# Starting a second attention with all rows of the first batch, and its loads in another order

## The reference

```
def _L1_xattn_ref(x, y, wq, bq, wk, bk, wv, bv, wo, bo):      # y: context, 8 x 120 x 384
    q = (x @ wq + bq).reshape(B, SQ, 16, 32)                  # x: layer norm of the rows
    k = (y @ wk + bk).reshape(B, SKV, 16, 32)
    v = (y @ wv + bv).reshape(B, SKV, 16, 32)
    scores = jnp.einsum('bqhd,bkhd->bhqk', q, k) / jnp.sqrt(32)
    attn = jax.nn.softmax(scores, axis=-1)
    out = jnp.einsum('bhqk,bkhd->bqhd', attn, v).reshape(B, SQ, 512)
    return out @ wo + bo
x = x + jnp.tanh(g_xattn[1]) * _L1_xattn_ref(_layernorm(x), ctx_768, ...)
```

## Time and profile before

| | us |
|---|---|
| median of 3 runs | 3957.67 (3955.93 to 3960.25) |
| the profiled execution | 3954.27 |
| its span | 3952.5 |
| TensorE busy | 3696.9 (94%) |
| VectorE busy | 2928.8 (74%) |
| ScalarE busy | 1903.4 (48%) |
| GpSimd busy | 1092.4 (28%) |
| mean granted TensorE clock | 0.97 |

### The profile page before, as it was taken

The page is one execution under the profiler, slowest core; times in us unless marked ns, Lnnn a source line. Parts: engine busy times, 40 slices in busy tenths (PEclk is TensorE's granted clock), DMA queues, the critical chain, the costliest instruction groups (busy, mean ns, idle before and its releaser), DMA issues. The chain is left out here.

```text
span 3952.5 us, 62618 instructions
## 1 busy us (share of the span) xinstructions
PE 3696.9 (94%) x21884; PEld 2919.7 (74%) x21884; DVE 2928.8 (74%) x4545; ACT 1903.4 (48%) x2703; POOL 1092.4 (28%) x1008
## 2 busy tenths in 40 slices
PE   7899999999899999999969999849999999999998
PEld 4556666566479888899955555549999999999997
DVE  5567766676668788787627888678888788888885
ACT  2555655565445555554415444414444444444443
POOL 2222211222001111111025665313333334333332
PEclk9999999999899999999979999959999999999999
DMA  4000010100257787776640221126777777786774
GB/s 160 29 32 16 27 35 30 32 13 17 80 177 265 247 288 245 272 260 211 203 141 30 72 91 54 54 76 208 236 239 235 222 221 236 234 241 207 238 233 128
DMA packets 386958, 596.53 MB, mean 151 GB/s; under 512 B 26559, under 2 KB 192511, under 8 KB 386559
## 3 DMA queue, kind: packets, MB, share of 16 engines
q1 hardware_dynamic: 352575, 521.68, 39.5%
q0 software_dynamic: 24864, 58.54, 6.7%
q10 hardware_dynamic: 9368, 14.33, 1.0%
HBM read 535.36 MB, written 59.12 MB: 150 GB/s over the span
## 5 line engine op out<-in xcount | busy, mean ns | idle before, releaser
L1282 DVE TENSOR_TENSOR e_all<-e_all_raw,e_WH 128x2048 fp32r<-128x2048 f32 x240 | 545.3, 2289 | 36.2 <-ACT e_WH L1276 36.2
L1441 PE MATMUL bank<-e_xh,e_WH 128*128 128x256 f32 x1984 | 563.2, 284 | 9.6 <-DVE e_xl L1313 5.4
L1441 PE MATMUL bank<-e_xh,e_all 128*128 128x256 f32 x1984 | 562.1, 283 | 0.0
L1441 PE MATMUL bank<-e_xl,e_WH 128*128 128x256 f32 x1984 | 562.0, 283 | 0.0
L1276 ACT ACTIVATE e_WH<-e_all_raw 128x2048 fp32r<-128x2048 f32 x240 | 458.1, 1910 | 188.6 <-DMA e_all_raw<-in_w 188.4
L1494 PE MATMUL bank<-e_WH,e_hh 128*128 128x512 f32 x1192 | 473.5, 397 | 0.0
L1494 PE MATMUL bank<-e_WH,e_hl 128*128 128x512 f32 x1192 | 468.3, 393 | 0.0
L1441 PEld LDWEIGHTS bank<-e_xh,e_WH 128*128 128x128 f32 x1984 | 379.0, 191 | 14.8 <-issue 13.0
L1441 PEld LDWEIGHTS bank<-e_xl,e_WH 128*128 128x128 f32 x1984 | 379.0, 191 | 0.9
L1441 PEld LDWEIGHTS bank<-e_xh,e_all 128*128 128x128 f32 x1984 | 378.9, 191 | 0.0
L1517 ACT ACTIVATE e_sil<-bank 128x256 f32<-128x256 f32 x248 | 95.2, 384 | 366.2 <-PE bank L1441 365.5
(11 more groups left out here) (380 smaller groups left out, 9213.8 us busy)
## 6 DMA issues: line engine op xcount, KB each, us to landing
e_all_raw<-in_w SPq DMA_DIRECT2D x320, 512.0 KB, 4.5
f_wl_raw<-in_w SPq DMA_DIRECT2D x120, 1024.0 KB, 5.6
e_all_raw<-in_w SPq DMA_DIRECT2D x80, 1024.0 KB, 5.3
e_rest_raw<-in_w SPq DMA_DIRECT2D x72, 1024.0 KB, 5.4
f_X<-in_x SPq DMA_DIRECT2D x32, 256.0 KB, 2.6
f_R<-in_x SPq DMA_DIRECT2D x32, 256.0 KB, 4.1
x<-f_R SPq DMA_DIRECT2D x32, 256.0 KB, 2.0
a_X<-x SPq DMA_DIRECT2D x32, 256.0 KB, 3.4
```

What stands on the lines that cost most here:

```text
L1282: dve.tensor_tensor(self.WL(p), self.raw(p), self.WH(p).bitcast(F32), ALU.subtract).then_inc(self.w_ready.sem, 1)
L1441: mm = nc.tensor.matmul(up[n % RING][:, q * ROWS:q * ROWS + ROWS], w, xx[:, c, :], start=(c == 0 and i == 0), stop=(c == DC - 1 and i == 2))
```

## The change

The first batch's rows are prepared in a prologue of their own on GpSimd (bias and root) and on VectorE (statistics and norm), ahead of the bodies; the tables then apply to batches 1 and up. SyncE issues bf, x of batch 0, wq, bq, kT, x of batch 1, V, bv, wo, gw, bo, and then the rest. `w_in` is split: `wq_in` (wq and bq) is waited for ahead of each q product on TensorE and each emptying of q on ScalarE, `wo_in` (wo, gw, bo) ahead of each output product on TensorE and, on GpSimd, ahead of the fold of bo, which moves from body -1 to body 0. The waits at the start of TensorE's and ScalarE's programs go.

```diff
@@ -1695,7 +1695,8 @@
 
-        w_in, kv_in, bf_in, folded, kzeroed = sem("weights_in"), sem("kv_in"), sem("bf_in"), sem("folded"), sem("kzeroed")
+        wq_in, wo_in, kv_in, bf_in, folded, kzeroed = \
+            sem("wq_in"), sem("wo_in"), sem("kv_in"), sem("bf_in"), sem("folded"), sem("kzeroed")
         k_ready = sem("k_ready")
@@ -1756,13 +1757,15 @@
                 load_x(0)
-                for dst, src in ((wq, "wq1"), (wo, "wo1"), (gw, "gw1")):
-                    sp.dma_start(dst[:, :, :], ins[src].rearrange("(c p) n -> p c n", p=P)).then_inc(w_in, 16)
-                sp.dma_start(bq[:, :], ins["bq1"]).then_inc(w_in, 16)
-                sp.dma_start(bo[:, :], ins["bo1"][None, :].to_broadcast([P, D])).then_inc(w_in, 16)
+                sp.dma_start(wq[:, :, :], ins["wq1"].rearrange("(c p) n -> p c n", p=P)).then_inc(wq_in, 16)
+                sp.dma_start(bq[:, :], ins["bq1"]).then_inc(wq_in, 16)
+                sp.dma_start(kT[:, :, :], k.kT1).then_inc(kv_in, 16)
+                load_x(1)
+                sp.dma_start(V[:, :, :], k.V1).then_inc(kv_in, 16)
                 sp.dma_start(bv[:, :], ins["bv1"]).then_inc(kv_in, 16)
-                sp.dma_start(kT[:, :, :], k.kT1).then_inc(kv_in, 16)
-                sp.dma_start(V[:, :, :], k.V1).then_inc(kv_in, 16)
+                for dst, src in ((wo, "wo1"), (gw, "gw1")):
+                    sp.dma_start(dst[:, :, :], ins[src].rearrange("(c p) n -> p c n", p=P)).then_inc(wo_in, 16)
+                sp.dma_start(bo[:, :], ins["bo1"][None, :].to_broadcast([P, D])).then_inc(wo_in, 16)
                 for n in bodies:
@@ -1770,7 +1773,7 @@
                                     .then_inc(x3_stored[t], 16)
-                    if -2 <= n < B - 3:
+                    if -1 <= n < B - 3:
                         load_x(n + 3)
@@ -1822,17 +1825,23 @@
 
+                for t in range(QT + 1):
+                    if t < QT:
+                        bias(0, t)
+                    if t:
+                        root(0, t - 1)
                 for n in bodies:
-                    if n == -1:
-                        pool.wait_ge(w_in, 16 * 5)
+                    if n == 0:
+                        pool.wait_ge(wo_in, 48)
                         pool.tensor_scalar(bo[:, :], bo[:, :], k.gate[:, 1:2], None, ALU.mult).then_inc(folded, 1)
...
                             root3(n - 1, NORM3_AT[s])
-                        if s in ROOT1_AT and 0 <= n + ROOT1_AT[s][0] < B:
+                        if s in ROOT1_AT and 0 < n + ROOT1_AT[s][0] < B:
                             root(n + ROOT1_AT[s][0], ROOT1_AT[s][1])
-                        if s in BIAS1_AT and 0 <= n + BIAS1_AT[s][0] < B:
+                        if s in BIAS1_AT and 0 < n + BIAS1_AT[s][0] < B:
                             bias(n + BIAS1_AT[s][0], BIAS1_AT[s][1])
@@ -1841,8 +1850,6 @@
             def _(pe):
-                pe.wait_ge(w_in, 16 * 5)
-
                 def scores(n, s):
@@ -1893,6 +1900,7 @@
                     elif kind == "q":
+                        pe.wait_ge(wq_in, 32)
                         for t in range(QT):
@@ -1903,6 +1911,7 @@
                     elif kind == "o":
+                        pe.wait_ge(wo_in, 48)
                         for c in range(DC):
@@ -1933,7 +1942,6 @@
                 act.wait_ge(kzeroed, 1)
-                act.wait_ge(w_in, 16 * 5)
 
@@ -1966,6 +1974,7 @@
                     elif kind == "q":
+                        act.wait_ge(wq_in, 32)
                         x = act.activation(qT[:, a, :], m, ACT.Identity, bias=bq[:, a:a + 1])
@@ -2066,6 +2075,11 @@
 
+                for t in range(QT + 1):
+                    if t < QT:
+                        add(0, t)
+                    if t:
+                        norm(0, t - 1)
                 for n in bodies:
@@ -2073,9 +2087,9 @@
                             norm3(n - 1, NORM3_AT[s])
-                        if s in NORM1_AT and 0 <= n + NORM1_AT[s][0] < B:
+                        if s in NORM1_AT and 0 < n + NORM1_AT[s][0] < B:
                             norm(n + NORM1_AT[s][0], NORM1_AT[s][1])
-                        if s in ADD_AT and 0 <= n + ADD_AT[s][0] < B:
+                        if s in ADD_AT and 0 < n + ADD_AT[s][0] < B:
                             add(n + ADD_AT[s][0], ADD_AT[s][1])
...
                             total(u)
```

## The result

The changed kernel takes 3942.53 us (median of 6 runs, 3939.57 to 3943.63) against 3957.76 (median of 6, 3955.93 to 3960.25): a ratio of 0.9962, 95% interval 0.9951 to 0.9973, or 15.2 us less by the medians. Forecast were 3945.0 and 12.7 us less. The profiled execution took 3940.56 us, 13.7 us less than that of before; its span of 3938.5 is 14.0 us shorter.

What follows compares the result with a forecast made beforehand. The stage's start was taken as bound by row 3's root queued behind a bias add awaiting the next batch's x. 14.2 gained minus 1.5 for the clock gave 12.7 us, from 3957.67 to 3945.0 us; range 3938.5 to 3951.5.

Steps and rivals of the forecast that it cites:

- Prologue: Stage start on GpSimd and VectorE: sixteen steps moved forward, root 3 ends at 2048.0, q starts at 2051.4, 15.8 us earlier.
- Loads: SyncE's queue at the stage start: V becomes the last arrival, taking 9.7 us, with bv landed at 2060.1.
- V is quick: Rival at the stage's loads: V lands 4.85 us earlier, q is last, scores gain 15.8 us, 3941.9 us; chance 0.13.
- Where the stall goes: ScalarE's key copies wait until 2060.1; first scores at 2063.5 against 2077.71, 14.2 us gained.
- The clock term: TensorE's pause from 2061.0 to 2063.5 lowers its clock: 1.5 us lost, bounds 0 and 3.4.
- The fold: Bo's fold at body 0 on GpSimd ends at 2065.5, covered before the first share: cost nothing, 1.58 us without cover.
- Waits: Added waits ahead of q and o on TensorE and on ScalarE: cost 0, upper bound 15 us.
- the slower rival: Waits ahead of q and o on TensorE cost 0.24 us each, 15.4 us for 64, giving 3960.4 us; chance 0.04.
- Given back later: Rival behind the stage's start: three more low-clock stretches return 10 of 12.7 us, 3951 to 3958 us; chance 0.08.

Runs made afterwards that it cites:

- the repetition: The changed kernel run again without any edit, in a later group of runs: 3941.4 us, ratio to before 0.9962.
- e1: The kernel before with the two prologues alone, its loads, their order and their one semaphore kept: 3946.19 us, ratio to before 0.9973.
- e6: The changed kernel with the fold of bo back in body -1 on GpSimd: 3949.0 us, ratio to before 0.9981.
- e8: As e4, with 80 filling transposes at the start and 8 or 9 ahead of later first-batch groups: 3940.22 us, ratio to before 0.9959.
- e10: As e8, with the third batch's x and bo loaded ahead of V and bo's fold at step 4 of body 0: 3937.23 us, ratio 0.9950.
- e5: The changed kernel with four more long-satisfied waits ahead of each of TensorE's 64 q and o groups: 3942.78 us, ratio to before 0.9969.
- e2: The changed kernel without the two prologues, keeping its loads, semaphores and late fold: 3942.03 us, ratio to before 0.9964.
- e3: The changed kernel with V and bv on their own semaphore, awaited only ahead of the first batch's PV: 3940.14 us, again 3939.51 us.
- e9: The changed kernel with V loaded as two DMAs of half the columns each: 3937.91 us in a single run.
- e4: As e3, with 56 filling transposes on TensorE at the start and 4 ahead of each first transpose group: 3939.3 us, ratio to before 0.9952.

## Why the prediction was right

**Prologue.** Root 3 was forecast at 14.3 after the first issue (2047.2) and measured at 14.2, q at 18.5 and measured at 18.65. The durations from the rows of before held: the norm beside GpSimd's add took 1.44 to 1.48, and the root 0.35 + 0.57. The norm at 2063.80 in the earlier trace rows is that of row 3, though the heading says row 2, and the statistics behind it are those of the next batch; the 1.9 us from its end to q were taken from the right norm.

**Loads.** kT was to land at 14.8 (2042.8 + 0.1 + 4.85, from 2032.93) and did at 14.2 (3.4 + 10.8); V at 27.1 and did at 26.65 (6.15 + 20.5). That the order of issue is the order of landing, and that V keeps its 10 us wherever it stands, were the assumptions, and both held in the changed kernel. "V is quick" fell: the last x row landed at 16.6 (issued at 2038.9, landed 10.9 later), V 10.1 us behind it. The term that was too small is bv: counted at 0.1, it came 0.6 behind V in the changed kernel (27.2) and 1.6 in the repetition (6.8 + 21.3 = 28.1), and it is what the key copies waited for. In the changed kernel the early V and the late bv cancel.

**Where the stall goes.** Key copies at 27.3 (forecast 27.2), first scores at 30.7 (30.6), 14.1 us gained (14.2). That they agree to 0.1 us is luck of this execution: in the repetition the key copies began at 28.2 and the scores at 31.6. The chain itself, V's group of loads, key copies, eviction, scores, is the one that was forecast. The ends of the range are a little wider than its own rivals and 3 us give (3938.9 and 3951.3), which changes nothing.

**The clock term** (1.5 us) was wrong in this execution: TensorE idled 2.79 us ahead of the first scores and the clock stayed up, q 2 took 3.70 us as before. In e1 it idled 3.70 and the clock fell behind it. TensorE's matmuls and table of stretches in e1, then the same of the changed kernel:

```profile
2065.14 1.08 PE L1866 MATMUL bank<-a_kcur,a_qT 64*128 64x240 f32 x8 [3.70 <-ACT a_qT L1974]
2066.15 5.40 PE L1904 MATMUL bank<-a_xT,a_wq 128*128 128x512 f32 x8
```

```profile
2065.00:2072.00 7.00, 6.86 (x22) 3.27 (x24) 6.01 (x9) 1.57 (x2) 6.13 (x8) 0.76 0.56 182
```

```profile
2064.00:2079.00 15.00, 12.16 (x56) 6.65 (x56) 13.22 (x19) 7.29 (x10) 10.01 (x11) 1.00 0.27 104
```

q 2 took 5.40 us there, 1.7 more. In e6 (idle for 3.58) it took the same 5.40; in the repetition (3.38) the clock stayed at 1.00. So the price was about right in size, but it wasn't paid here. The low stretch of before that it was taken from (2090 to 2100) is there again in the changed kernel, at the same step and behind a pause of 3.00 us as before. Without the term the forecast would have been 3943.5, 1 us from the median instead of 2.5.

**The fold.** "Cost nothing, cover: the first share" held, and e6 and e8 show what it rests on. But I had priced the loss of the cover at the fold's own 1.58, and it costs 6.5 in e6, while e10 gets 3.0 back from e8. What counts is not the fold but the five or six row steps queued behind it and VectorE's steps that wait for those.

**Waits.** Nothing that can be told, as forecast; the slower rival is out by e5.

**Given back later.** The profiles don't show it: 1874.8 us from the first scores to the end before, 1874.6 after.

**What the prediction did not see** is that the two halves do the same thing. It gave the gain to the prologue. Of the loads it counted only V's landing, 1.0 us sooner than before by their new order (2061.1 to 2060.1), as the bound that takes 1.6 back. The row that waited would have been early by the loads alone: the earlier trace rows and the 1.3 us of one bias add would have told that, and e2 shows it. For e1, too, V's landing gives the start (31.5 by the expectation, 32.0 measured). The sum was right since V with bv is the later bound, or level with q, whichever half is there.

## What to carry to other kernels

When an engine's program interleaves the preparation of the next item with that of the first, ask which loads the next item's steps wait for: a load that comes too late for the *second* item can set the start of the first, and moving the load and moving the step are two cures of one wait. Work out for the moved start what lands last, and what each wait that was moved holds up behind it, on the next engine too; the wait itself is the smaller part of its price. Once a start is bound by a landing, freeing the compute ahead of it brings next to nothing (the changed kernel against e2) until the landing's wait goes (e3), and then the next cover is gone (e8, e10).

## What the runs showed of the hardware

- A load of 2 KB in 128 pieces (bv), issued right behind one of 1920 KB, landed 0.6 to 2.0 us after it in the changed kernel, its repetition, e2 to e6 and e9. In e8 and e10, where TensorE runs the longer filling, it landed 4.3 and 4.2 us after it, and there also 1.1 us behind wo, a load issued after it (e8: bv at 30.8, wo at 29.7): in those two the order of issue was not the order of landing. Why is open.
- V (120 partitions x 16 KB) moved at 199 to 230 GB/s with the DMA engines busy, kT (128 x 15 KB) at about 400; with V split the key copies began at 26.6 and 26.9, with V in one piece at 27.0 to 28.2.
- The same norm on VectorE took 0.52 to 0.55 us with no bias add of GpSimd beside it and 1.42 to 1.48 with one (before and changed kernel).
- Ahead of the first scores, TensorE's clock fell behind idle times of 3.6 and 3.7 us (e6, e1) and stayed up behind 2.8 and 3.4 (changed kernel, its repetition). The length of a pause alone doesn't decide: a later pause, of 3.0 us in each of four kernels, ahead of transposes of the next batch, was followed by the low clock in before, the changed kernel and its repetition (granted clock 0.50 in the changed kernel from 2081 to 2083), but not in e10 (1.00 from 2074 to 2085). Short transposes with pauses of up to 1.4 us between groups kept it at 2.4 GHz (e8). In e4 the groups were shorter, with pauses of 3.1 and 1.2 us, and the clock was at 0.50 from 2047 on; the two were not varied apart.
